# The last stage of an expert layer and a mixing layer on one core: order of y and the low parts on VectorE, and where TensorE waits for the low part

## What is computed

```
x = x + _L0_ffn_ref(_L0_cond_ref(...), ...)      # experts: mean of the two chosen rows
# _L1_cond_ref: a 32 x 32 matrix per sequence, mixed from 8 kernels by attention weights
agg_w = jnp.einsum('bk,koi->boi', att, weight[..., 0])
out = jnp.einsum('boi,bih->boh', agg_w, x) + agg_b[:, :, None]
# _L1_ffn_ref: W = scales * q - zeros, q unpacked from 4-bit numbers
out = jnp.einsum('bsi,io->bso', x, W) + bias
x = x + ...
```

## Time and profile before

| | us |
|---|---|
| median of 3 runs | 547.59 |
| lowest and highest run | 547.28, 550.64 |
| the profiled execution's own time | 549.46 |
| its span | 547.7 |
| TensorE busy in the span | 519.4 (95%) |
| VectorE busy | 339.4 (62%) |
| ScalarE busy | 121.8 (22%) |
| mean granted TensorE clock | 0.978 |

### The profile page before, as it was taken

How to read it: one execution, slowest core, us unless ns; L and a number is a source line. 1 busy time by engine, 2 the same in 40 slices (tenths; PEclk the granted TensorE clock), 3 DMA queues, 4 the chain that set the end, 5 groups by cost and what they waited for, 6 DMA issues and landing times. The chain is left out here.

```text
span 547.7 us, 10445 instructions
## 1 busy us (share of the span) xinstructions
PE 519.4 (95%) x2486; PEld 349.3 (64%) x2487; DVE 339.4 (62%) x1003; ACT 121.8 (22%) x277; POOL 144.0 (26%) x162
## 2 busy tenths in 40 slices
PE   6969999999979999999999999999968999999996
PEld 5969999999956444444444444444436667777774
DVE  3466888888873653333333333334753699999996
ACT  2122223324410111111111111111131222222221
POOL 8042444444462000000000000000006655555520
PEclk9999999999978999999999999999988899999999
DMA  4999778887344844444444444444476788888852
GB/s 114 378 312 343 249 251 277 291 281 258 139 166 155 214 159 154 153 153 153 153 153 153 153 153 153 153 153 154 138 247 180 222 277 288 279 278 287 294 183 96
DMA packets 84823, 114.32 MB, mean 209 GB/s; under 512 B 15197, under 2 KB 51853, under 8 KB 83509
## 3 DMA queue, kind: packets, MB, share of 16 engines
q1 hardware_dynamic: 57936, 56.49, 33.0%
q0 software_dynamic: 10528, 33.75, 18.1%
q10 hardware_dynamic: 16328, 23.72, 12.3%
HBM read 67.48 MB, written 46.45 MB: 208 GB/s over the span
## 5 line engine op out<-in xcount | busy, mean ns | idle before, releaser
L989 PE MATMUL bank<-we,hT 128*128 x536 | 230.8, 593 | 1.2 <-DVE hT L815 1.2
L989 PEld LDWEIGHTS bank<-we,hT 128*128 128x128 f32 x536 | 101.5, 190 | 129.4 <-issue 129.2
L454 POOL DMA_INDIRECT we<-result_d,gidx x64 | 65.4, 1021 | 292.0 <-issue 288.5
L824 DVE TENSOR_TENSOR ring_a<-bank,be_bc 128x512 f32<-128x512 f32 x71 | 48.9, 690 | 125.5 <-PE bank L989 116.2
L957 PE MATMUL bank<-wconv,phases 128*128 128x128 f32 x768 | 94.2, 281 | 4.8 <-issue 4.1
L957 PEld LDWEIGHTS bank<-wconv,phases 128*128 128x128 f32 x768 | 91.4, 197 | 5.3 <-issue 4.3
L532 ACT ACTIVATE ring_b<-ring_a 128x512 f32<-128x512 f32 x71 | 44.9, 632 | 206.7 <-DVE ring_a L824 200.0
L435 POOL DMA_INDIRECT lists_d<-htok,row_i x64 | 62.9, 982 | 87.8 <-issue 63.4
L815 DVE STREAM_TRANSPOSE hT<-htok 128x512 f32<-128x512 f32 x71 | 49.9, 702 | 8.3 <-DMA htok<-lists_d 8.3
L1029 PE MATMUL bank<-mix_bd,we 128*128 128x128 f32 x256 | 36.7, 288 | 4.6 <-DVE we L868 3.4
L1029 PEld LDWEIGHTS bank<-mix_bd,we 128*128 128x128 f32 x256 | 32.0, 196 | 11.2 <-DVE we L868 10.0
(11 more groups left out here) (164 smaller groups left out, 410.8 us busy)
## 6 DMA issues: line engine op xcount, KB each, us to landing
htok<-lists_d SPq DMA_DIRECT2D x284, 64.0 KB, 2.4
result_d<-ring_b ACTq DMA_DIRECT2D x71, 256.0 KB, 2.5
xt<-in_x SPq DMA_DIRECT2D x64, 256.0 KB
we<-in_L_ffn_W_e SPq DMA_DIRECT2D x8, 1024.0 KB
out<-orow SPq DMA_DIRECT2D x32, 256.0 KB
lists_d<-orow SPq DMA_DIRECT2D x8, 256.0 KB
be_bc<-in_L_ffn_b_e ACTq DMA_DIRECT2D x1, 2048.0 KB
rows_r<-ctx_d SPq DMA_DIRECT2D x1, 1920.0 KB, 10.9
```

The lines of the kernel that those rows point to most:

```text
L454: pool.indirect_dma_start(found[:, j, k, :], None, result_d, bass.IndirectOffsetOnAxis(ap=gidx[:, j, k:k + 1], axis=0), bounds_check=NT * ...
L824: dve.tensor_tensor(ring_a[:, j % 2, :], ps_exp[j % 2][:, :], be_bc[:, bass.ds(expert, 1), :].rearrange("p a n -> p (a n)"), ALU.add).then ...
L989: mm = pe.matmul(ps_exp[j % 2][:, :], hT[:, j % 2, p * P:(p + 1) * P], we[:, bass.ds(expert, 1), p, :].rearrange("m a n -> m (a n)"), star ...
```

## The change

VectorE's step is reordered: output (843), first half of y (854, now line 849), scaling (848, now 854), second half of y (868, now 858), low part of the correction (859, now 864), low part of the tile (864, now 869). TensorE waits for `high_ready` ahead of the four products with high, and for `low_ready` only between them and the four products with low. No arithmetic is added or removed.

```diff
@@ VectorE, step3
-                if live(c, NG):
-
-                    wait(dve, lin_done, c + 1)
-                    scaled = ps_lin[c % U][:, :]
-                    dve.tensor_tensor(scaled, scaled, scale_bc[:, :], ALU.mult).then_inc(scaled_ready, 1)
                 if live(a, NG):
 
                     wait(dve, x3_in[ja], ring_count(a, ja, XR))
                     wait(dve, gathered[ja], (a - ja) * (32 // U) + 32)
                     wait(dve, out_ready, a - 3)
                     dve.tensor_tensor(y_t[:, ja, :], xt[:, ja, :], found[:, ja, 0, :], ALU.add).then_inc(ya_ready, 1)
+                if live(c, NG):
+
+                    wait(dve, lin_done, c + 1)
+                    scaled = ps_lin[c % U][:, :]
+                    dve.tensor_tensor(scaled, scaled, scale_bc[:, :], ALU.mult).then_inc(scaled_ready, 1)
+                if live(a, NG):
+                    wait(dve, ya_ready, a + 1)
+                    wait(dve, terms_done, a - 1)
+                    dve.scalar_tensor_tensor(y_t[:, ja, :], y_t[:, ja, :], 1.0, found[:, ja, 1, :], ALU.mult, ALU.add,
+                                             accum_out=ysum[:, ja % 2:ja % 2 + 1]).then_inc(y_ready, 1)
                 if live(g, NG):
 
                     wait(dve, thigh_ready, g + 1)
...
-                if live(a, NG):
-                    wait(dve, ya_ready, a + 1)
-                    wait(dve, terms_done, a - 1)
-                    dve.scalar_tensor_tensor(y_t[:, ja, :], y_t[:, ja, :], 1.0, found[:, ja, 1, :], ALU.mult, ALU.add,
-                                             accum_out=ysum[:, ja % 2:ja % 2 + 1]).then_inc(y_ready, 1)
@@ TensorE, step3
+                    wait(pe, high_ready, g + 1)
+                    wait(pe, out_ready, g - 3)
+                    for q in range(PH):
+                        pe.matmul(ps_lin[j][:, :], high[:, j % 2, q * P:(q + 1) * P], wq[:, q, :],
+                                  start=(q == 0), stop=False, skip_group_check=True)
                     wait(pe, low_ready, g + 1)
-                    wait(pe, out_ready, g - 3)
-                    for h, half in enumerate((high, low)):
-                        for q in range(4):
-                            mm = pe.matmul(ps_lin[j][:, :], half[:, j % 2, q * P:(q + 1) * P], wq[:, q, :],
-                                           start=(h == q == 0), stop=(h == 1 and q == 3), skip_group_check=True)
+                    for q in range(PH):
+                        mm = pe.matmul(ps_lin[j][:, :], low[:, j % 2, q * P:(q + 1) * P], wq[:, q, :],
+                                       start=False, stop=(q == PH - 1), skip_group_check=True)
```

More of the change, by code:

```diff
@@ L843, in step3 @@
                     dve.tensor_tensor(orow[:, jd % 2, :], ps_lin[jd][:, :], y_t[:, jd, :], ALU.add).then_inc(out_ready, 1)
+                if live(a, NG):
+                    wait(dve, x3_in[ja], ring_count(a, ja, XR))
+                    wait(dve, gathered[ja], (a - ja) * (32 // U) + 32)
+                    wait(dve, out_ready, a - 3)
+                    dve.tensor_tensor(y_t[:, ja, :], xt[:, ja, :], found[:, ja, 0, :], ALU.add).then_inc(ya_ready, 1)
                 if live(c, NG):
```

## The result

The changed kernel takes 545.87 us (median of 10 runs, 543.97 to 547.38), the kernel before 548.03 beside it. The ratio is 0.9944, with a 95% interval from 0.9925 to 0.9964: 3.1 us less. Two more comparisons of the same kernel gave 0.9959 (0.9933 to 0.9986) and 0.9935 (0.9909 to 0.9961). The forecast was 6.4 us less and a range whose upper end was 545.7, so it was wrong in size: the direction is right, but under half of the gain came, and the time lies just outside the range. A gain under about 1% is what the prediction called no change, with a chance of 0.31. The profiled execution has a span of 543.2 against 547.7.

What follows compares the result with a forecast made beforehand. The prediction took a loop of mutual waits between TensorE and VectorE as the bound; 4.4 us from the pace plus 2.0 from the stage's start made 6.4, so 547.59 - 6.4 = 541.2 us, range 539.3 to 545.7.

Steps and rivals of the forecast that it cites:

- the loop: Last stage: TensorE and VectorE wait for each other, 7.42 us per two tiles; y 0.92 earlier makes it 6.50.
- VectorE's own step: VectorE in the last stage: same seven operations after the change, so 3.53 us a tile.
- from tile 5 to tile 31: Last stage's steady part: 26 steps at 3.54 us instead of 96.40 us in all, 4.36 us saved.
- The Trainium skill's rule on partitions: VectorE: operands in another partition group start only once earlier work has finished; step estimated at about 3.44 us.
- TensorE's own step: TensorE in the last stage: 3.20 + 0.34 = 3.54 us a tile without waiting for y.
- The new wait among the eight products: TensorE's added wait on the first low weight load: taken as 0, at most 0.40 us a tile.
- The low part's cover: Low part made last on VectorE, before TensorE's four low matmuls need it: 1.5 us remain.
- Rival D: TensorE's added wait stops early weight loading, up to 0.40 us a tile: slower, 553.6 us; chance 0.04.
- Rival B: Floor above 3.54: VectorE's step 3.65 or an exposed load's 0.10 on TensorE (3.64); 544.0 us, chance 0.12.
- C: DMA is the bound in the last stage, only the start's 2.0 us remain: 545.6 us; chance 0.06.
- A: TensorE's clock returns sooner at the stage's start, 1.2 us more saved: 540.0 us; chance 0.12.
- The start, 2.0 us: Last stage's start: tile 5's mixing at 438.21 instead of 440.21, saving 2.0 us once.

Runs made afterwards that it cites:

- pe_only: Kernel before with only TensorE's new waits, VectorE's old order kept: ratio 0.9993 to the kernel before.
- before_swap: Kernel before with the first half of y directly behind the output and the scaling third, y still last: ratio 1.0055 to the kernel before.
- ring8: Changed kernel with eight slots for y instead of four: ratio 0.9914 to the kernel before; again 0.9867; with five idle matmuls added 0.9888.
- start_only: Kernel before with VectorE's new order in the first four steps of the stage only: ratio 0.9982 to the kernel before, repeated 0.9994.
- before_ring8: Kernel before with a ring of eight tiles for y and nothing else: ratio 0.9997 to the kernel before.
- before_warm: Kernel before with seven idle matmuls between the sums of tile 0 and the mixing of tile 1: ratio 1.0023 to the kernel before.
- dve_only: Kernel before with VectorE's new order alone, TensorE's old waits kept: ratio 0.9964 to the kernel before.
- swap: Old VectorE order with only its last two operations exchanged, plus TensorE's new waits: ratio 0.9935 to the kernel before.
- scale_first: Changed kernel with the scaling back between output and first half of y: 543.06 us, ratio 0.9903 to the kernel before; repeated 543.02 us, 0.9891.

## Why the prediction was wrong in size

**What bounds, and the loop: right.** The loop of 7.42 us for two tiles set the pace. With y ahead of the two low parts it no longer does: the alternation is gone, and so is line 843's wait. pe_only leaves both as they were, before_swap lengthens the loop by 0.23 where 0.20 was expected of it, and the pace by 0.12 where 0.10 was.

**VectorE's own step: the step that failed.** The prediction had "the same seven operations, so 3.53" and weighed only the 0.72 ahead of line 859, from 3.42 to 3.65. Measured: 3.67. Without the wait VectorE's own distances come to 3.46 in ring8, where TensorE is the bound. The error is that a moved operation's waits were taken as met, because they had been met before. The new pace, "the larger of 3.54 and 3.53", was therefore VectorE's 3.67 and not TensorE's. The list of instructions ahead of the prediction even names `out_ready` on line 849, directly under the operation that sets it. The term "from tile 5 to tile 31" should have been 26 x (3.71 - 3.67) = 1.0, and measured 96.40 - 95.24 = 1.2, against 4.36 forecast. The prediction's own sign of being wrong, "VectorE without any gap and a step above 3.6", is what the trace shows.

**The Trainium skill's rule on partitions: it fits.** The 0.72 in front of line 859 became 0.61 in front of the scaling, and line 864 starts 0.11 behind the short read. By the rule VectorE's step was estimated at 3.44; ring8's own distances give 3.46. So the estimate from the Trainium skill (VectorE: DVE Perf Modes, Two Vector instructions with no wait between them) was nearer than the 3.53 taken in the sum. Neither holds the wait of line 849, which is no matter of partitions.

**TensorE's own step, 3.54: right.** ring8 runs at 3.52. The changed kernel starts its tiles 3 to 6 at that pace, until VectorE has no lead left.

**The new wait among the eight products: right at nothing.** No bracket stands at the first low load, in the changed kernel or in pe_only. Rival D is out.

**The low part's cover: there, but smaller.** The forecast had 1.5 us to spare. The low part starts at 481.08 and takes 0.69, and the low loads start at 482.48: 0.7 remain, for VectorE runs later behind TensorE when it is itself the bound. In ring8, where TensorE is the bound, 1.4 remain.

**Rival B was the case that came**: forecast at 3.65 with 544.0, held 0.12 likely. Its mechanism there was another, the neighbours' distance. That 3.65 lies near 3.67 is luck. C didn't come: no wait for gathers shows up in the steady part, at a DMA share of 0.89 in 500 to 520. A came in its condition and not in its time. No low clock falls into the start part of the three executions of the changed kernel, where the kernel before had one, yet the time is 545.9 and not 540.0. That the change did this isn't shown, for before_swap, with y last, has none there either.

**The start, 2.0 us: in part.** By difference 3.1 - 1.2 = 1.9 us of the measured gain lie outside the pace from tile 5 on, which looks like the forecast. The agreement is in part luck, for the forecast's 2.0 has three parts.

- 0.54 came from y(1) ahead of low(0). That is shown: from tile 0's to tile 1's mixing are 2.52 to 2.87 us in the twelve executions with the low part last, and 3.17 to 3.33 in the five with y last.
- 1.12 came from y(3) no longer standing behind a cast that was late in one execution. Eight of the seventeen executions have no late cast, before_swap among them, which has y last. A wait of one execution was put into the median of all.
- 0.34 was pace, the two steps behind tile 3. start_only lacks it, and it came as 0.5.

start_only, which has the first two parts alone, gains 0.3 to 1.0 us with intervals that reach 0. With the 0.5 that makes 0.8 to 1.5 of the 1.9, and the interval of the whole gain (2.0 to 4.1 us) is wider than the rest. What the rest is stays open.

**The late casts.** Casts between 425 and 443 us came late in the executions of the kernel before, pe_only, before_ring8, before_warm, dve_only, swap and the three of ring8, and in none of the three of the changed kernel, the two of scale_first, the two of start_only and the one of before_swap. The profile's views name no releaser, but the semaphore records do: every late cast but one, whose record is missing, starts 0.02 us behind the update of the semaphore that TensorE's matmul sets for it. In the kernel before the cast is this one:

```profile
430.82 0.59 ACT L561 CAST high<-bank 128x512 fp32r<-128x512 f32 x1 [2.48 <-remote]
```

`mixed_done` is updated at 430.79, and the mixing's last matmul is recorded as ended at 429.20. In the eight executions without late casts all 32 of these updates come 0.01 behind that end. So it is TensorE's update that comes late. Whether its matmul was done late (matmul ends are modelled in the profile) or only told late, and why, isn't shown. The same nine traces hold 9,600 to 9,791 semaphore updates, the eight others 11,927 to 11,951, for nearly the same instructions. So the recording itself may have a part in it, and no run here separates that.

## What to carry to other kernels

When an operation is moved, its waits are part of the move: write down for each which instruction meets it, and how many instructions now lie between the two. A wait for the operation directly ahead on the same engine shows no idle bracket; it shows as a start-to-start distance longer than the same operation has elsewhere (0.81 against 0.60 here). When two engines are within 0.01 us of each other as the next bound, add up the second one's distances in the new order, pair by pair, before taking the old sum.

## What the runs showed that wasn't expected

A wait on VectorE for the operation directly ahead cost 0.20 to 0.21 us behind the output operation (which reads the product's bank), but only 0.11 between the halves of y. The reason for the difference wasn't tried.

Late casts on ScalarE, most of them 1 to 5 us late, appear at the stage's start in nine executions here and not in the eight others. Each follows a late semaphore update of TensorE's. The start part of these nine is 16.6 to 24.5 us, that of the eight others 16.3 to 18.7. The difference is more than the change itself gives, so one profiled execution against another says little about the start.
